# First marks by a scan and 32x32 transposes on DVE, spread over the partitions by small DMAs from two queues

## The reference

```python
inter = xf @ c1_w.T @ c2_w.T                 # rank 16, 1792 columns
blk = inter.reshape(tokens, 56, 32)
idx = jnp.argmax(blk, axis=-1) + jnp.arange(0, 1792, 32)
h = relu(einsum('bkm,bm->bk', w1[idx], xf))  # one of 32 rows in each block
out = einsum('bk,bkm->bm', h, w2t[idx])
```

## Time and profile before

| | |
|---|---|
| median of 3 runs | 1007.56 us (1005.65 to 1009.1) |
| profiled execution, own time | 998.58 us |
| its span, first to last instruction | 996.8 us |
| mean granted TensorE clock | 0.944 |
| busy: PE, DVE, ACT, POOL | 908.2, 562.4, 442.9, 193.1 us |

### The profile page before, as it was taken

How to read it: one execution, slowest core, us unless ns; L and a number is a source line. 1 busy time by engine, 2 the same in 40 slices (tenths; PEclk the granted TensorE clock), 3 DMA queues, 4 the chain that set the end, 5 groups by cost and what they waited for, 6 DMA issues and landing times. The chain is left out here.

```text
span 996.8 us, 12134 instructions
## 1 busy us (share of the span) xinstructions
PE 908.2 (91%) x4472; PEld 533.0 (53%) x4472; DVE 562.4 (56%) x743; ACT 442.9 (44%) x821; POOL 193.1 (19%) x183
## 2 busy tenths in 40 slices
PE   5868999999899998999989975999999999999995
PEld 3745543333334333343333434777777777777774
DVE  4636567888656885468866533545563365326413
ACT  3302466777654775456765542322222222222231
POOL 6302003730210002100021002333321222122221
PEclk8889999999989998599988978999999999999998
DMA  8466535643342243323433124214030002001101
GB/s 249 160 205 240 169 110 159 175 123 91 91 117 69 76 134 80 97 85 79 135 82 109 34 97 102 82 44 155 14 116 11 1 3 103 2 1 43 42 1 42
DMA packets 50858, 92.99 MB, mean 93 GB/s; under 512 B 5648, under 2 KB 13840, under 8 KB 50288
## 3 DMA queue, kind: packets, MB, share of 16 engines
q1 hardware_dynamic: 49312, 87.05, 29.3%
q0 software_dynamic: 1488, 5.16, 1.9%
HBM read 56.80 MB, written 34.87 MB: 92 GB/s over the span
## 5 line engine op out<-in xcount | busy, mean ns | idle before, releaser
L509 DVE TENSOR_REDUCE neg_max<-ps_max 128x2 f32<-128x1024 f32 x256 | 302.9, 1217 | 90.1 <-PE ps_max L670 89.7
L486 ACT ACTIVATE probs<-ps_st 128x512 f32<-128x512 f32 x496 | 270.2, 595 | 142.6 <-PE ps_st L707 139.7
L707 PE MATMUL ps_st<-q,k 50*128 50x512 f32 x496 | 181.9, 511 | 28.5 <-ACT probs L486 27.6
L707 PEld LDWEIGHTS ps_st<-q,k 50*128 50x128 f32 x496 | 71.9, 192 | 203.1 <-ACT probs L486 156.8
L670 PE MATMUL ps_max<-k,q 48*128 48x512 f32 x512 | 152.8, 452 | 14.0 <-DVE neg_max L509 9.2
L721 PE MATMUL ps_pv<-probs,v 128*32 128x512 f32 x1024 | 147.3, 649 | 5.9 <-ACT probs L486 2.3
L978 POOL TENSOR_TENSOR g_l<-picked,g_h 128x512 fp32r<-128x512 f32 x56 | 73.1, 1306 | 286.9 <-ACT g_h L1017 286.9
L1003 ACT ACTIVATE mask_t<-ps_t 128x512 bf16<-128x512 bf16 x56 | 33.4, 597 | 163.6 <-PE ps_t L1199 163.6
L1211 PE MATMUL ps_h<-xt_h,w_h 128*128 128x512 f32 x224 | 93.8, 419 | 8.0 <-ACT relu L1010 8.0
L1073 DVE TENSOR_REDUCE top<-ps_prep 128x14 f32<-128x448 f32 x62 | 38.6, 623 | 99.0 <-PE ps_prep L1188 98.8
L670 PEld LDWEIGHTS ps_max<-k,q 48*128 48x128 f32 x512 | 75.6, 199 | 28.9 <-DVE neg_max L509 13.5
(11 more groups left out here) (159 smaller groups left out, 1141.2 us busy)
## 6 DMA issues: line engine op xcount, KB each, us to landing
q_stacks<-parts SPq DMA_DIRECT2D x48, 256.0 KB
q<-q_stacks SPq DMA_DIRECT2D x64, 192.0 KB, 3.6
sums<-stage SPq DMA_DIRECT2D x32, 256.0 KB, 3.4
k<-k_stacks SPq DMA_DIRECT2D x64, 96.0 KB, 3.1
x_raw<-xT SPq DMA_DIRECT2D x16, 256.0 KB, 8.5
yf<-after_attention SPq DMA_DIRECT2D x4, 1024.0 KB, 5.3
w_raw<-w POOLq DMA_DIRECT2D x16, 224.0 KB, 3.1
w_raw<-w SPq DMA_DIRECT2D x14, 256.0 KB, 2.9
```

Source lines behind the costliest of these rows:

```text
L486: nc.scalar.activation(probs[kt % 2][:, r], score_bank(n, r), ACT.Exp, scale=float(HD) ** -0.5).then_inc(exp_done, 1)
L509: nc.vector.tensor_reduce(neg_max[n % 2][:, i // 2, :, i % 2], ps_max[i % 2][:], AX.X, ALU.max, negate=True).then_inc(max_red, 1)
L707: nc.tensor.matmul(score_bank(n, r), k_[n % QR][64 * a:64 * a + ROWS, kt * P:(kt + 1) * P], q[n % QR][64 * a:64 * a + ROWS, j, :], start=T ...
```

## The change

- After is_equal (now into `equal`, 128x448 bf16), DVE makes a scan over the chunk: `rank = doubling x previous + equal`, where `doubling` is 2, and 0 at the first column of each block of 32. rank is then 1 at the first maximum of a block and 2, 4, ... at later columns. A DVE transpose turns its 32x32 blocks into `turned`.
- The 32x32 blocks stand in the wrong partitions, so DMAs from SBUF to SBUF spread them into `rank_t` (inner columns in the partitions): 16 DMAs for a chunk, one for each of 4 offsets and 4 groups of 32 partitions, each 32 partitions x 3 or 4 blocks x 256 bytes. Two groups are issued by SyncE, two by ACT's own queue, after slots 1, 5, 7 (round 0: 8) and 12 (round 0: 13) of `high_g`; chunk 0 of round 0 ahead of everything of the slots.
- `pick` compares rank_t with 1 and multiplies in place. TensorE's transposes and `first_marks`, ACT's `turn`, and the constants `first` and `ident16` are gone.
- u's columns are written in another order of tokens (`_by_group`, `_in_order`), which makes runs of 128 tokens fit the transposed blocks.
- ps_h and ps_prep each have two banks. w2's raw tiles lie where w2_l (and wo_l) will be, and w2's load waits for what the split waited for.

```diff
+        def spread_ranks(eng, b, c, groups):
+            i = b * NC + c
+            first, last = c * CH // BLK, (c + 1) * CH // BLK
+            eng.wait_ge(rank_turned, TT * (i + 1))
+            if b:
+                eng.wait_ge(picked_ready, (b - 1) * MT + (last - 1) // 4 + 1)
+            for o in range(4):
+                blocks = [n for n in range(first, last) if n % 4 == o]
+                m = slice(blocks[0] // 4, blocks[-1] // 4 + 1)
+                for g in groups:
+                    src = turned[i % 2][BLK * g:BLK * (g + 1), blocks[0] - first:blocks[-1] - first + 1:4]
+                    eng.dma_start(rank_t[BLK * o:BLK * (o + 1), m, P * g:P * (g + 1)],
+                                  src.rearrange("p n t k -> p n (t k)")).then_inc(rank_in[i % 2], DMA)
+
+        def spread_at(eng, b, m, groups):
+            at = (1, 5, 7 if b else 8)
+            if m in at:
+                spread_ranks(eng, b, at.index(m) + 1, groups)
+            if b + 1 < NB and m == (12 if b else 13):
+                spread_ranks(eng, b + 1, 0, groups)
...
             for r in range(REP):
                 sp.dma_start(att[:, r], last.rearrange("(g r h d t) -> r h g d t", r=REP, g=NKV, h=2, d=HD)[r, 0]
                              ).then_inc(att_in, DMA)
+            spread_ranks(sp, 0, 0, (0, 1))
...
             def relu(b, m):
                 i = b * MT + m
                 act.wait_ge(h_done, i + 1)
                 if i >= 2:
-                    act.wait_ge(picked_ready, i - 1)
-                nc.scalar.activation(act_r[m % 2][:], ps_h[:], ACT.Relu).then_inc(relu_ready, 1)
+                    act.wait_ge(g_ready, i - 1)
+                nc.scalar.activation(picked[m % 2][:], ps_h[i % 2][:], ACT.Relu).then_inc(relu_ready, 1)
...
-            turn(0, 0)
             high_w2(0)
+            spread_ranks(act, 0, 0, (2, 3))
             for b in range(NB):
                 for m in range(MT):
                     if b == 0 and m + 1 < MT:
                         high_w2(m + 1)
                     relu(b, m)
-                    if b * MT + m + 1 < NB * MT:
-                        turn(*divmod(b * MT + m + 1, MT))
                     high_g(b, m)
+                    spread_at(act, b, m, (2, 3))
...
                     nc.vector.tensor_tensor(
-                        mask[:, t, c * CH:(c + 1) * CH].rearrange("p (n k) -> p n k", k=BLK), src,
+                        equal[:].rearrange("p (n k) -> p n k", k=BLK), src,
                         top[t % 2][:].rearrange("p (n o) -> p n o", o=1).broadcast_to([P, CH // BLK, BLK]),
                         ALU.is_equal).then_inc(prep_done, 1)
 
+                    dve.wait_ge(prep_done, n + 1)
+                    if i == 0 and t == 0:
+                        dve.wait_ge(doubling_set, 1)
+                    nc.vector.tensor_tensor_scan(rank[:], doubling[:], equal[:], 0.0, ALU.mult, ALU.add
+                                                 ).then_inc(rank_done, 1)
+                    dve.wait_ge(rank_done, TT * i + t + 1)
+                    if i >= 2 and t == 0:
+                        dve.wait_ge(rank_in[i % 2], 16 * DMA * (i // 2))
+                    nc.vector.transpose(turned[i % 2][:, :, t], rank[:].rearrange("p (n k) -> p n k", k=BLK)
+                                        ).then_inc(rank_turned, 1)
+
             def pick(b, m):
-                i = b * MT + m
-                dve.wait_ge(z_done, i + 1)
+                i, c = b * MT + m, b * NC + chunk_of(m)
+                dve.wait_ge(rank_in[c % 2], 16 * DMA * (c // 2 + 1))
                 dve.wait_ge(relu_ready, i + 1)
-                if i >= 2:
-                    dve.wait_ge(g_ready, i - 1)
-                nc.vector.scalar_tensor_tensor(picked[m % 2][:], ps_z[:], 1.0, act_r[m % 2][:], ALU.is_equal,
+                nc.vector.scalar_tensor_tensor(picked[m % 2][:], rank_t[:, m], 1.0, picked[m % 2][:], ALU.is_equal,
                                                ALU.mult).then_inc(picked_ready, 1)
...
-                    first_marks(b, m)
...
-                    if b * MT + m + 1 < NB * MT:
-                        turn_mask(*divmod(b * MT + m + 1, MT))
```

More of the change, by code:

```diff
@@ L341, in _ @@
             nc.gpsimd.memset(ident[:], 0.0).then_inc(constants, 1)
-            nc.gpsimd.memset(first_f[:], 0.0).then_inc(constants, 1)
-            pool.wait_ge(constants, 2)
+            pool.wait_ge(constants, 1)
             nc.gpsimd.affine_select(out=ident[:], in_=ident[:], compare_op=ALU.not_equal, fill=1.0, base=0,
                                     pattern=[[-1, P]], channel_multiplier=1).then_inc(constants, 1)
[L347 to L360, removed]
             nc.gpsimd.memset(neg_half[:], -0.5).then_inc(powers_set, 1)
@@ L652, in turn_v @@
                 if b == 0:
-                    pe.wait_ge(constants, 8)
+                    pe.wait_ge(constants, 2)
                 if 0 < b < NB - 1:
@@ L807, in _feed_forward @@
 def _feed_forward(nc, x, x1, out, w2, sums, rden, keep):
-    w1_h, w1_l, c1_h, c1_l, c2_s, ident, ident16, first, xt_h, xt_l, u, wo_h, wo_l = keep
+    w1_h, w1_l, c1_h, c1_l, c2_s, ident, xt_h, xt_l, u, wo_h, wo_l, w2_late = keep
     att_h, att_l = xt_h[1], xt_l[1]
@@ L822, in _feed_forward @@
         w2_h = sb("w2_h", [P, W2_OWN, D], F32R)
+        with ExitStack() as under:
+            w2_raw = under.enter_context(nc.sbuf_tensor("w2_raw", [P, W2_OWN, D], F32))
         w2_l = sb("w2_l", [P, W2_OWN, D], F32R)
@@ L826, in _feed_forward @@
         den, inv_den = sb("den_last", [P, P]), sb("inv_den_last", [P, P])
-        w2_raw = [sb(f"w2_raw{j}", [P, D]) for j in range(2)]
         x_sb = [sb(f"xf_sb{j}", [P, D]) for j in range(2)]
         top = [sb(f"top{j}", [P, CH // BLK]) for j in range(2)]
-        mask = sb("mask", [P, TT, INTER], BF16)
-        mask_t = [sb(f"mask_t{j}", [P, S], BF16) for j in range(2)]
-        act_r = [sb(f"relu{j}", [P, S]) for j in range(2)]
+        equal, rank = sb("equal", [P, CH], BF16), sb("rank", [P, CH], BF16)
+        doubling = sb("doubling", [P, CH], BF16)
+        turned = [sb(f"turned{j}", [P, CH // BLK, TT, BLK], BF16) for j in range(2)]
+        rank_t = sb("rank_t", [P, MT, S], BF16)
         picked = [sb(f"picked{j}", [P, S]) for j in range(2)]
@@ L1043, in _, with step @@
         def _(dve):
-            def step(kind, b, s, bank):
+            def step(kind, b, s):
                 n = number(b, s, kind)
-                half = halves(n)
+                half, bank = halves(n), ps_prep[n % 2]
                 dve.wait_ge(prep_mm, n + 1)
@@ L1118, in _ @@
             for t in range(TT):
-                step("prep", 0, marks(0, t), (ps_prep, ps_z)[t % 2])
+                step("prep", 0, marks(0, t))
                 if t == 1:
@@ L1161, in _, with step @@
         def _(pe):
-            def step(kind, b, s, bank, banks=1):
+            def step(kind, b, s):
                 n = number(b, s, kind)
-                if n >= banks:
-                    pe.wait_ge(prep_done, n - banks + 1)
+                bank = ps_prep[n % 2]
+                if n >= 2:
+                    pe.wait_ge(prep_done, n - 1)
                 if kind == "wo":
@@ L1190, in step @@
                 last.then_inc(prep_mm, 1)
-            def turn_mask(b, m):
-                i = b * MT + m
-                pe.wait_ge(prep_done, number(b, marks(-(-(m + 1) * P // CH) - 1, TT - 1)) + 1)
-                if i:
-                    pe.wait_ge(mask_t_ready, i)
-                for t in range(TT):
-                    last = nc.tensor.transpose(ps_t[:, t * P:(t + 1) * P], mask[:, t, m * P:(m + 1) * P], ident16[:])
-                last.then_inc(mask_turned, 1)
             def inner_up(b, m, ks):
@@ L1210, in inner_up @@
                     for n, (w, xx) in enumerate(((w1_h, xt_h), (w1_h, xt_l), (w1_l, xt_h))):
-                        last = nc.tensor.matmul(ps_h[:], w[:, k, m * P:(m + 1) * P], xx[b % 2][:, k],
+                        last = nc.tensor.matmul(ps_h[i % 2][:], w[:, k, m * P:(m + 1) * P], xx[b % 2][:, k],
                                                 start=(k == 0 and n == 0), stop=(k == KT - 1 and n == 2))
@@ L1214, in inner_up @@
                     last.then_inc(h_done, 1)
-            def first_marks(b, m):
-                i = b * MT + m
-                pe.wait_ge(mask_t_ready, i + 1)
-                if i:
-                    pe.wait_ge(picked_ready, i)
-                nc.tensor.matmul(ps_z[:], first[:], mask_t[m % 2][:], start=True, stop=True).then_inc(z_done, 1)
             def inner_down(b, m, ts):
@@ L1241, in _ @@
             for t in range(TT):
-                step("prep", 0, marks(0, t), (ps_prep, ps_z)[t % 2], 2)
+                step("prep", 0, marks(0, t))
                 if t % 2:
                     inner_up(0, 0, (t - 1, t))
-            pe.wait_ge(prep_done, TT)
-            turn_mask(0, 0)
             for b in range(NB):
@@ L1253, in _ @@
                     if steps:
-                        step(*steps[0], ps_prep)
```

(2 more changed lines are left out.)

78 lines of the change are left out of this document (44 added, 34 removed).

## The result

The changed kernel took 1047.36 us (median of 4 runs, 1041.35 to 1054.79), beside 1006.61 us for the kernel before: a ratio of 1.042, 95% interval 1.033 to 1.051. The forecast was 1021 with a range up to 1042. The direction was right, the size was three times too small: 40 us in place of 13.7, and the time lies above the range.

The account below looks back on a forecast made before the run. TensorE was taken to set the pace, except at the start, where DMAs do. Round 0 +8.3, later rounds +1.4 and clock +4 made +13.7, on the earlier median 1007.56 giving 1021 us, range 996 to 1042.

Parts of the forecast that it names:

- a step of marks: On DVE, reduce, is_equal, scan and transpose together: 3.05 us, where it was 1.3; bounds 2.4 and 5.
- The start: From the first reduce at 593.71 through blocks, reciprocals and w2's third tile: ps_out of tile 1 8.6 us late, tile 2 12.3.
- g(1): Tile 1's g ready for ps_out: at 631.4 in round 0, at 16.7 us into a later round.
- g(2): Tile 2's g ready for ps_out: at 641.4 in round 0, 12.3 us late; at 26.35 us into a later round.
- ScalarE is free of chunk 1 at 22.8: In a round, ScalarE's issues for chunk 1 end before DVE reaches pick(2), so at 0.63 us each they cost nothing.
- The list of signs: What the trace should show, among it relu behind ScalarE's issues in slots 2, 6 and 8, scan near 1.1 us.
- much slower: Rival: queues hinder each other at 1.0 us an issue, relu late at three chunks a round; about +30, 1050; chance 0.17.
- slots 4 to 13 give back 4.7: In round 0 after the start, ten slots each save 0.47 us, leaving round 0 at +7.6.
- Waits of 1.5, 2.85 and 0.85: In a round, TensorE's waits for g(1), g(2) and g(3); with 0.7 for bank and add 5.9 us, against 6.6 saved.
- the 1.3 of the forecast: TensorE's clock may fall in slots 3 and 4 of a round, costing 1.3 us a round, +4 in all.
- 0.7 us for such a meeting: A DVE step right behind a pick meets GpSimd's g_l: 0.7 us at the start, 1.4 a round.

Follow-up runs that it names:

- e1: Changed kernel with ScalarE issuing no DMA, half of the squares left out and half of rank_t constant: 1033.38 us, ratio 1.029.
- e6: e4 with SyncE issuing 12 of 16 squares and ScalarE 4 a slot later, except for chunks wanted soon: 1031.41 us, ratio 1.024.
- e2: Changed kernel with all sixteen DMAs of a chunk issued by SyncE, none by ScalarE: 1053.33 us, ratio 1.049.
- e4: Changed kernel with w2's tiles 2 to 5 loaded at the start, ahead of the first squares: 1042.46 us, ratio 1.038.
- e9: e7 with w2's last tiles ahead of chunk 3's squares (shared 8 to 8), and round 1's first chunk 1 marks in round 0's slot 13: 1006.31 us.
- e7: e6 with chunk 1's marks for rounds 2 and 3 moved into the round before, its squares there shared 12 to 4: 1012.78 us, ratio 1.007.
- e3: Changed kernel without the scan, the transposes moving `equal`, so every maximum is marked: 1007.87 us, ratio 1.0037.

## Why the prediction missed

**Right.** The prices. Scan 1.09 us alone (forecast 1.1), transpose 0.65 with its gap (0.65), a step of marks 3.0 us (3.05) and 3.6 where GpSimd runs beside it (3.05 + 0.7). An issue is 0.60 us in the median on SyncE and 0.63 on ScalarE, and in a row of eight ScalarE's take 0.65 to 0.84 each (0.63; two of sixteen rows are above 0.75), a landing 1.9 us (2). The start down to its first link:

```profile
630.13 0.02 POOLq L1011
630.14 0.02 issue
630.16 1.26 POOL g_l L1012
...
641.22 1.59 POOL g_l L1012
...
649.35 1.59 POOL g_l L1012
...
662.04 1.28 POOL g_l L1012
```

g(1) ends at 631.42, forecast 631.4; g(2) at 642.8, forecast 641.4. A slot without steps even gained 0.60 us, 0.13 more than the forecast, some 7 us in 56 slots that came unforeseen: the costs were missed by more than the times differ.

**Wrong, first: what stands behind ScalarE's eight issues.** The step was "ScalarE is free of chunk 1 at 22.8, before DVE comes to pick(2), so at 0.63 us its queue hides; above about 0.75 us it does not". It was worked for chunk 1 alone, and there it held. In round 1 relu stood 8.56 us behind the issues, of which the pick saw 0.45:

```profile
761.98 0.60 ACT L1036 ACTIVATE picked<-ps_h 128x512 f32<-128x512 f32 x1 [8.56 <-issue]
```

```profile
762.68 0.69 DVE L1123 SCALAR_TENSOR_TENSOR picked<-rank_t,picked 128x512 f32<-128x512 bf16 x1 [0.45 <-ACT picked L1036]
```

The list of signs has relu behind its issues in slots 6 and 8 too, but the sum has no term for them. Chunks 2, 3 and the next chunk 0 have a way of their own: last transpose, 5.4 us of issues (6.4 in the rows below), relu, pick, g_h, g_l. The chain shows it between slots 12 and 13 of round 1:

```profile
827.10 0.04 DVE turned L1115
827.14 0.53 issue
827.67 0.66 DVE picked L1123
...
834.22 0.62 ACTq L904
...
834.95 0.61 ACT picked L1036
...
835.65 0.69 DVE picked L1123
```

From one pick's start at 827.67 to the next at 835.65 are 8.0 us, in a slot that could take 5.5. That is one half of the rival "much slower", relu held at three chunks of each round, at issues of 0.63 us in the median and not at the 0.75 from which I had let it decide. Its condition was wrong: removing the issues gave 21 us (e1), and 11.5 came back by moving twelve of sixteen issues off ScalarE where there was no hurry (e6). The other half, that the queues get in each other's way at 1.0 us an issue, did not occur. That its 1050 lies near the measured 1047 is chance: much of the 40 us is the scan's and w2's.
The Trainium skill (Perfetto Trace Analysis, DMA Instruction, HWDGE) has the descriptor generator locked for one sequencer at a time. The rows of e2 and of the changed kernel above don't show it at that size: two queues together issued sixteen in 5.58 us, one alone in 10.38. What there is of holding up is some 0.26 us in most batches (5.43 against 5.17). Single longer issues, up to 1.87 us, occur with one queue too (1.83 in e2).

**Wrong, second: "slots 4 to 13 give back 4.7".** In round 0 they lost, 3.7 us from slot 4 to slot 13, and slot 4 was late already. Slot 4's g_l came 19.5 us late, since ScalarE waited 10.11 us for w2's sixth tile behind the load of y on SyncE's queue (rows of e4). I had followed that queue to the third tile only. w2's order was worth 15.1 us (e4); the forecast held the first wait and not the second.

**Wrong, third: the sum over a round.** "Waits of 1.5, 2.85 and 0.85 ... sum 5.9 against 6.6 saved" took each round to start with DVE level with TensorE. It does not: round 1's pick(0) waits for the blocks of a chunk whose last marks stand in slot 13 of round 0:

```profile
742.49 0.69 DVE L1123 SCALAR_TENSOR_TENSOR picked<-rank_t,picked 128x512 f32<-128x512 bf16 x1 [4.71 <-DMA rank_t<-turned]
...
746.74 2.45 DVE L1130 TENSOR_TENSOR yf<-ps_out,yf 128x512 f32<-128x512 f32 x4
```

and the add behind it frees TensorE's bank late. TensorE:

```profile
747.54 0.76 PE L1250 MATMUL ps_out<-w_h,g_h 128*128 128x512 f32 x1 [5.14 <-DVE yf L1130]
748.10 0.63 PE L1250 MATMUL ps_out<-w_l,g_h 128*128 128x512 f32 x1
748.53 0.63 PE L1250 MATMUL ps_out<-w_h,g_l 128*128 128x512 f32 x1
...
752.21 0.39 PE L1250 MATMUL ps_out<-w_h,g_l 128*128 128x512 f32 x1
752.44 0.39 PE L1235 MATMUL ps_h<-xt_h,w_h 128*128 128x512 f32 x1
```

The granted clock in this stretch (windows, columns as in the earlier trace rows):

```profile
742.00:747.00 5.00, 0.40 (x2) 0.00 (x0) 4.40 (x6) 1.11 (x2) 1.26 (x1) 0.77 0.07 28
747.50:751.50 4.00, 3.96 (x10) 3.18 (x11) 3.93 (x6) 0.00 (x0) 0.00 (x0) 0.50 0.00 0
752.00:756.00 4.00, 4.00 (x19) 3.35 (x18) 3.90 (x6) 0.63 (x1) 1.28 (x1) 1.00 0.01 2
```

Behind 5.1 us of idling the clock is at 0.50, the level of 1.2 GHz, and matmuls follow each other at 0.43 us, 4 us later at 0.23. Nine at 0.20 us more are 1.8 us, near the 1.3 of the forecast; but there are 22 waits of TensorE, not one in a round, and how much the clock took of the 46 us no run separates.

**The scan's share.** Its 1.1 us was in the sum, at the right price, and yet taking it out gave 41 us, as much as the whole loss. e9, and e7 in part, show one side: in slots 0 to 3 DVE's work is on the path. The other side is argued from the chain above: at the end of a chunk the scan makes the last transpose late, and with it ScalarE's issues. A price of 1.1 us paid 64 times is 70 to 84 us; I let it count only at the start and where slots 0 and 1 overflow. Where the 41 us lie can be read by comparing the lateness of e3 with the changed kernel's: 5.0 us by slot 1 of round 0, 8.8 in the rest of that round, 17.0 in slots 0 to 4 of rounds 1 to 3 and 10.4 in their slots 5 to 13.

**What stays open.** The clock's share; how much of the scan's 41 us is DVE's own load and how much its part in making ScalarE's issues late; what GpSimd's contention costs as a whole (the scan's mean of 1.309 against 1.09 alone is 64 x 0.22 = 14 us of DVE's time, not all of it on the path).

## What to carry to other kernels

When DMA issues are given to a compute engine, follow every batch of them, not the tightest alone, from what it waits for to the instruction behind it and on to the engine that sets the pace; here 5.4 us ahead of a relu, which the sum had at nothing for three chunks of each round, cost 21 us, half as much as the scan. And an operation's price says little without the slots in which the engine has no room: 84 us of scans cost 41 us of time, over half of it at the start and in slots 0 to 4 of a round. Follow an in-order queue past the first item that you care about: one load that waits early holds all behind it. And where a stage has waits at several places, their cures may add up (77.6 against 75.3 us here), or two may cover each other in one slot, as w2's tile, ScalarE's issues and x's load did in slots 9 and 10: then curing one shows only the next.

## What the runs showed of the hardware

- The scan is sensitive to what GpSimd does. In the start of the changed kernel, alone, beside a running subtraction of GpSimd, and in e7 right behind a pick:

```profile
595.32 1.09 DVE L1110 TENSOR_TENSOR_SCAN rank<-doubling,equal 128x448 bf16<-128x448 bf16 x1
...
598.29 1.51 DVE L1110 TENSOR_TENSOR_SCAN rank<-doubling,equal 128x448 bf16<-128x448 bf16 x1
```

```profile
748.25 1.75 DVE L1138 TENSOR_TENSOR_SCAN rank<-doubling,equal 128x448 bf16<-128x448 bf16 x1
```

  GpSimd's subtractions ran from 597.60 to 598.86 and from 747.76 to 749.05; both scans ended 0.94 to 0.95 us behind them, as if they had hardly run until then. The prediction had 0.7 us for such a meeting; here it is 0.42 and 0.66. The norms went from 540 to 710 ns. 448 bf16 elements in 1.09 us against 0.65 for their transpose, with a fixed 0.15 us in each (an estimate from the 623 and 691 ns of the earlier trace rows), are 0.94 against 0.50 us and agree with half throughput for the scan, as the Trainium skill states (DVE: opcode table, instruction layouts, handler registers and perf-mode slots, section 6).
- Twelve matmuls took 2.72 us in the changed kernel and 2.79 to 2.80 before, with nothing between them in either. Why was not tried.
- The time at which attention, unchanged, ends differs by 11 us between executions, more than most of the effects studied here; only stages measured from a mark inside the trace can be compared.
